# A fused Macaron block (FFN, ReLU attention, FFN) on one core: new step tables for TensorE, ScalarE, VectorE and GpSimd

## The reference

```python
x = x + 0.5 * _L0_ffn_ref(_layernorm(x), ...)      # "pre"
x = x + _L0_attn_ref(_layernorm(x), ...)           # attention, 16 heads of 8
x = x + 0.5 * _L0_ffn_ref(_layernorm(x), ...)      # "post"
# _L0_ffn_ref(x):  h = LN(x)*g + b; y = silu(h @ w1 + b1); return x + 0.5*(y @ w2 + b2)   128 -> 512 -> 128
# _L0_attn_ref(x): w = relu(q k' / sqrt(8)); attn = w / (sum(w) + 1e-6); out = (attn @ v) @ w_out + b_out
#                  return LN(x + out) * gamma + beta
```

## Time and profile before

| | |
|---|---|
| time, median of 3 runs | 376.71 us (376.18 to 376.83) |
| the profiled execution | 376.2 us, of which the span of its instructions is 374.4 us |
| PE busy | 359.7 us (96% of the span) |
| DVE, ACT, POOL busy | 279.4, 232.9, 217.7 us |
| one batch in the middle (batch 3) | 43.57 us |

### The profile page before, as it was taken

How to read it: one execution, slowest core, us unless ns; L and a number is a source line. 1 busy time by engine, 2 the same in 40 slices (tenths; PEclk the granted TensorE clock), 3 DMA queues, 4 the chain that set the end, 5 groups by cost and what they waited for, 6 DMA issues and landing times.

```text
span 374.4 us, 11752 instructions
## 1 busy us (share of the span) xinstructions
PE 359.7 (96%) x4518; PEld 182.1 (49%) x4518; DVE 279.4 (75%) x689; ACT 232.9 (62%) x425; POOL 217.7 (58%) x447
## 2 busy tenths in 40 slices
PE   8999999999999999999999999999999999999997
PEld 8844433543435544454435544455434544352376
DVE  6776678797588965888577975889658785668774
ACT  3477466656766476756777377664767567667533
POOL 7694156489734887167763787358871557014541
PEclk9999999999999999999999999999999999999999
DMA  7016006300640017200361006400270003600001
GB/s 204 10 33 167 3 6 167 83 3 2 146 108 5 3 56 165 63 4 31 77 151 30 4 28 134 122 3 3 58 194 6 2 30 70 156 4 32 0 2 60
DMA packets 14103, 22.66 MB, mean 61 GB/s; under 512 B 2528, under 2 KB 3808, under 8 KB 14048
## 3 DMA queue, kind: packets, MB, share of 16 engines
q1 hardware_dynamic: 11456, 17.83, 19.7%
q10 hardware_dynamic: 2592, 4.07, 3.3%
HBM read 3.54 MB, written 2.10 MB: 15 GB/s over the span
## 4 chain that ended last, share of the span: by engine, by line
PE 80%; DVE 10%; ACT 4%; issue 3%; POOL 2%; DMA 1%; SPq 0%; ACTq 0%; POOLq 0%; DVEq 0%
PE o_bank L685 27%; PE scores L662 13%; PE pre_bank L603 10%; PE post_bank L603 9%; DVE probs L1283 4%; PE pre_bank L608 4%; PE post_bank L608 3%; PE pre_bank L609 2%; PE pre_bank L631 2%; PE pre_bank L596 2%; PE post_bank L631 2%; PE post_bank L609 1%; PE o_bank L590 1%; ACT post_y L873 1%; ACT pre_y L873 1%
## 5 line engine op out<-in xcount | busy, mean ns | idle before, releaser
L1283 DVE TENSOR_SCALAR probs<-scores 128x512 f32<-128x512 f32 x242 | 155.1, 680 | 60.5 <-PE scores L662 56.4
L984 ACT ACTIVATE probs<-scores 128x512 f32<-128x512 f32 x262 | 141.4, 595 | 84.5 <-PE scores L662 83.2
L685 PE MATMUL o_bank<-probs,v_op 128*32 128x512 f32 x1024 | 135.8, 602 | 0.2
L662 PE MATMUL scores<-q_op,k_op 32*128 32x512 f32 x504 | 72.4, 494 | 0.8 <-ACT probs L984 0.2
L662 PEld LDWEIGHTS scores<-q_op,k_op 32*128 32x128 f32 x504 | 29.0, 181 | 72.9 <-issue 58.5
L685 PEld LDWEIGHTS o_bank<-probs,v_op 128*32 128x32 f32 x1024 | 22.3, 108 | 27.4 <-issue 23.9
L603 PEld LDWEIGHTS post_bank<-w,post_y 128*32 128x32 f32 x960 | 26.5, 110 | 12.9 <-issue 12.6
L603 PE MATMUL post_bank<-w,post_y 128*32 128x128 f32 x960 | 31.6, 273 | 0.1
L1312 POOL TENSOR_SCALAR norm_y_var<-norm_y_mv 128x4 f32<-128x4 f32 x7 | 1.4, 199 | 50.5 <-DVE norm_y_mv L1054 50.5
L603 PE MATMUL pre_bank<-w,pre_y 128*32 128x128 f32 x960 | 30.8, 274 | 0.0
L603 PEld LDWEIGHTS pre_bank<-w,pre_y 128*32 128x32 f32 x960 | 25.7, 110 | 8.1 <-issue 7.6
(11 more groups left out here) (219 smaller groups left out, 553.6 us busy)
## 6 DMA issues: line engine op xcount, KB each, us to landing
k_op<-k_parts SPq DMA_DIRECT2D x62, 128.0 KB, 2.6
q_op<-q_parts SPq DMA_DIRECT2D x62, 128.0 KB, 2.7
out_dram<-o_rows ACTq DMA_DIRECT2D x7, 256.0 KB, 2.0
pre_x<-in_x_dram ACTq DMA_DIRECT2D x6, 256.0 KB, 2.6
w_int<-in_L_ffn_fc_q_dram SPq DMA_DIRECT2D x2, 256.0 KB, 4.0
rows<-in_lines_dram ACTq DMA_DIRECT2D x1, 256.0 KB, 7.2
s_rows<-in_L_ffn_fc_scales_dram SPq DMA_DIRECT2D x1, 256.0 KB, 6.9
wqk<-in_w_qk_dram SPq DMA_DIRECT2D x1, 256.0 KB, 6.9
```

The costliest lines, as they stand in the source:

```text
L662: mm(score_bank(b, s, i, j), k_op[rows, g, P * kt:P * (kt + 1)], q_op[rows, g, :], start=True, stop=True).then_inc(scores_done[i], 1)
L685: last = mm(o_bank[pair][VW * j:VW * (j + 1), :], v_op[:, kt, heads_of(g).start + 2 * j, :], probs[:, s % 2, j, :], start=(odd == 0 and kt ...
L984: activation(probs[:, s % 2, 2 * i + j, :], score_bank(b, s, i, j), ACT.Relu).then_inc(probs_done[i][j], 1)
L1283: v.tensor_scalar(probs[:, s % 2, 2 * i + j, :], score_bank(b, s, i, j), 0.0, None, ALU.max).then_inc(probs_done[i][j], 1)
```

## The change

The matmuls and the instructions of all other engines do the same work; what changes is their order, and two waits. The tables of batches 2 to 6 (`*_ORDER`):

- PE: `fc1.1`, `fc1.2`, `fc1.3` of pre and `fc2.0` stand behind V instead of between S and V; `post.op` stands behind V and ahead of `fc1.2`; post's `fc1.2` has step 13 alone, `v` moves from step 13 to 14, and post's `fc1.3` from between S and V of step 14 to behind V of step 15.
- POOL: `x_stats` and `x_apply` of the rows after next stand behind `uT`; `post.xr`, which stood behind `uT`, stands ahead of it; `pre.xr` stands ahead of `v_in`. DVE makes its part of `x_stats` in step 10 instead of 4.

Batch 1 gets tables of its own for PE, ACT and DVE (`*_SECOND`): the same, with `post.hT` in step 8 and `post.fc1.0` to `fc1.3` in steps 9, 10, 12 and 14. The last batch does post's `fc2` in steps 0 and 1 instead of 3 to 6, ahead of `op`, and `out` and the store with it. There `op` waits for fc2's drained bank, and fc2 no longer waits for `y`.

```diff
+PE_SECOND = [
...
+    ([], ["post.hT@-1"]),
+    ([], ["post.fc1.0@-1"]),
...
 PE_ORDER = [
     ([], ["pre.fc1.0@1"]),
-    (["pre.fc1.1@1"], []),
-    (["pre.fc1.2@1", "post.op@-1"], []),
...
+    ([], ["pre.fc1.1@1"]),
+    ([], ["post.op@-1", "pre.fc1.2@1"]),
...
 PE_END = [
+    ([], ["post.fc2.0@-2"]),
+    (["post.fc2.1@-2", "post.fc2.2@-2", "post.fc2.3@-2"], []),
+    ([], ["post.op@-1"]),
...
+DVE_SECOND = [
...
+    ["oT.0", "den.0"],
+    ["post.hT@-1"],
...
 DVE_END = [
     [],
-    ["oT.1@-1", "den.1@-1", "a.1@-1", "aT@-1"],
+    ["oT.1@-1", "den.1@-1", "a.1@-1", "post.out@-2", "aT@-1"],
...
     [],
+    ["post.xr@-1"],
+    ["pre.uT@1"],
+    ["pre.x_stats@2"],
     ["pre.x_apply@2"],
-    ["pre.uT@1"],
-    ["post.xr@-1"],
-    ["pre.x1_beta@1"],
+    ["pre.x1_beta@1", "pre.xr@2"],
     ["v_in.0@1", "v_in.1@1"],
-    ["pre.xr@2"],
     [],
 ]
...
-def of_batch(b, start, order, end):
-
-    return start if b == 0 else end if b == B - 1 else order
+def of_batch(b, start, second, order, end):
+
+    return start if b == 0 else second if b == 1 else end if b == B - 1 else order
...
                         next_fill(st, b, "fc2")
-                        if st is post:
+                        if st is post and b < B - 3:
 
                             pe.wait_ge(y_done, b + 2)
...
-                            pe.wait_ge(post.free, len(POST_FILLS) * (b - 1) + post.n("fc1.3"))
+                            last_use = "fc2" if b == B - 2 else "fc1.3"
+                            pe.wait_ge(post.free, len(POST_FILLS) * (b - 1) + post.n(last_use))
```

More of the change, by code:

```diff
@@ L70 @@
 ]
+PE_SECOND = [
+    ([], ["pre.fc1.0@1"]),
+    ([], ["pre.fc1.1@1"]),
+    ([], ["post.op@-1", "pre.fc1.2@1"]),
+    ([], ["pre.fc1.3@1"]),
+    ([], ["pre.fc2.0@1"]),
+    (["pre.fc2.1@1"], ["pre.fc2.2@1"]),
+    (["pre.fc2.3@1"], []),
+    ([], []),
+    ([], ["post.hT@-1"]),
+    ([], ["post.fc1.0@-1"]),
+    (["pre.uT@1"], ["post.fc1.1@-1"]),
+    ([], ["pre.k@1"]),
+    ([], ["pre.q@1", "post.fc1.2@-1"]),
+    ([], ["pre.v@1"]),
+    ([], ["post.fc1.3@-1"]),
+    (["pre.hT@2"], []),
+]
 PE_ORDER = [
     ([], ["pre.fc1.0@1"]),
-    (["pre.fc1.1@1"], []),
-    (["pre.fc1.2@1", "post.op@-1"], []),
-    (["pre.fc1.3@1"], []),
-    (["pre.fc2.0@1"], ["pre.fc2.1@1"]),
+    ([], ["pre.fc1.1@1"]),
+    ([], ["post.op@-1", "pre.fc1.2@1"]),
+    ([], ["pre.fc1.3@1"]),
+    ([], ["pre.fc2.0@1", "pre.fc2.1@1"]),
     (["pre.fc2.2@1", "pre.fc2.3@1"], []),
@@ L84 @@
     ([], ["pre.q@1", "post.fc1.1@-1"]),
-    ([], ["pre.v@1", "post.fc1.2@-1"]),
-    (["post.fc1.3@-1"], []),
-    (["pre.hT@2"], []),
+    ([], ["post.fc1.2@-1"]),
+    ([], ["pre.v@1"]),
+    (["pre.hT@2"], ["post.fc1.3@-1"]),
 ]
@@ L141 @@
 ]
+ACT_SECOND = [
+    ["pre.fc1.0@1"],
+    ["pre.fc1.1@1"],
+    ["pre.fc1.2@1", "pre.load_x@2"],
+    ["pre.fc1.3@1"],
+    ["post.y_apply@-1"],
+    [],
+    [],
+    [],
+    ["post.hT@-1"],
+    ["post.fc1.0@-1"],
+    ["pre.uT@1", "post.fc1.1@-1"],
+    ["pre.k@1"],
+    ["pre.q@1", "post.fc1.2@-1"],
+    ["pre.v@1"],
+    ["post.fc1.3@-1"],
+    ["pre.hT@2"],
+]
 ACT_ORDER = [
@@ L155 @@
     ["pre.q@1", "post.fc1.1@-1"],
-    ["pre.v@1", "post.fc1.2@-1"],
-    ["post.fc1.3@-1"],
-    ["pre.hT@2"],
+    ["post.fc1.2@-1"],
+    ["pre.v@1"],
+    ["pre.hT@2", "post.fc1.3@-1"],
 ]
@@ L162 @@
     [],
-    [],
+    ["post.store@-2"],
     [],
@@ L167 @@
     ["post.y_apply@-1"],
-    ["post.store@-2"],
+    [],
     [],
@@ L205 @@
 ]
+DVE_SECOND = [
+    ["oT.1@-1", "den.1@-1"],
+    ["a.1@-1", "aT@-1"],
+    ["post.y@-1", "post.y_stats@-1"],
+    [],
+    [],
+    ["post.x2@-1", "post.x2_stats@-1"],
+    ["pre.x1@1"],
+    ["pre.x1_stats@1"],
+    ["oT.0", "den.0"],
+    ["post.hT@-1"],
+    ["a.0", "pre.x_stats@2"],
+    ["pre.k_lo@1"],
+    ["pre.q_lo@1"],
+    [],
+    [],
+    ["pre.hT@2"],
+]
 DVE_ORDER = [
@@ L210 @@
     [],
-    ["pre.x_stats@2"],
+    [],
     ["post.x2@-1", "post.x2_stats@-1"],
@@ L216 @@
     ["post.out@-2"],
-    ["a.0"],
+    ["a.0", "pre.x_stats@2"],
     ["post.hT@-1", "pre.k_lo@1"],
@@ L231 @@
     [],
-    ["post.out@-2"],
+    [],
     ["post.x2@-1"],
@@ L840, in _ @@
             for b in range(B):
-                for s, (early, late) in enumerate(of_batch(b, PE_START, PE_ORDER, PE_END)):
+                for s, (early, late) in enumerate(of_batch(b, PE_START, PE_SECOND, PE_ORDER, PE_END)):
                     step_scores(b, s)
@@ L975, in _ @@
             for b in range(B):
-                for s, beside in enumerate(of_batch(b, ACT_START, ACT_ORDER, ACT_END)):
+                for s, beside in enumerate(of_batch(b, ACT_START, ACT_SECOND, ACT_ORDER, ACT_END)):
                     if STEPS * b + s - 1 > 0:
@@ L1274, in _ @@
             for b in range(B):
-                for s, beside in enumerate(of_batch(b, DVE_START, DVE_ORDER, DVE_END)):
+                for s, beside in enumerate(of_batch(b, DVE_START, DVE_SECOND, DVE_ORDER, DVE_END)):
                     if STEPS * b + s - 1 > 0:
```

## The result

The changed kernel takes **384.39 us** (median of 4 runs, 383.27 to 390.37) against 376.6 us of the kernel before beside it; the ratio is **1.020** (95% interval 1.017 to 1.022). Ratios leave out two runs as slow ones: the 390.37 us here, whose granted clock was lower than that of the others, and one of 797.15 us among the twelve of experiment 6. It is slower by 7.8 us, where I had forecast 2.4 and a range that ended at 381.3. The profiled execution takes 384.3 us.

The account below looks back on a forecast made before the run. PE, busy 96% of the span, bounds the kernel, so only its waits can change. Batches 2 to 6 +4.35, batch 1 -1.0 and last batch -1.0 sum to +2.4 us on 376.71: 379.1 us, range 376.4 to 381.3.

Parts of the forecast that it names:

- the sum of step 11: Batches 2 to 6: k's new wait for POOL's low part +1.89, post's fc1.0 wait gone -0.44, restart +0.10: +1.55 us each.
- an overlap of the four large instructions with `a_t`: POOL's post.xr beside DVE's a_t: low part 0 to 0.2 us later per batch, up to +1 us in all; 0 taken.
- Batch 1: Its own tables leave 3.2 to 3.4 of 4.3 us of waits: -1.0 us, bounds -4.0 and +1.
- wait for post's low part: Batch 1: post's fc1.0, one step behind post's hT, makes PE wait some 1.6 us for DVE's low part.
- The last batch: fc2 in steps 0 and 1 covers evictions, about 1.5 us go, 1.1 come back: net -1.0 us, bounds -2 and +1.
- both silu waits: Batches 2 to 6: with quarters behind V, pre's and post's fc1 no longer wait for silu, -0.5 us each.
- the wait of k: Step 11, batches 2 to 6: PE's L755 waits for POOL's pre_t_lo, 1.5 to 2 us each.
- hT behind `v`: Batches 2 to 5: v one S ahead of hT, which waits for ACT to copy v, +0.4 us each.
- a forecast of 44.5: Sign to look for: a middle batch takes 44.5 us instead of 43.57, batch 6 a little shorter.
- The low part was not in time: Rival, chance 0.08: POOL's low part is in time, step 11 at most its old length, 371.3 us.
- nearly all its waits: Rival, chance 0.12: batch 1 loses nearly all its waits (-4.0), 376.1 us, no difference to be told.
- the bound in the middle: Rival, chance 0.12: evictions bound steps 15 to 3, 0.3 us for two steps in each batch, 382.1 us.

Follow-up runs that it names:

- experiment 6: The kernel before with the changed kernel's batch 1 tables alone, POOL's order and DVE's x_stats in step 4 as they were: 376.29 us, ratio 0.999.
- Experiment 3: The changed kernel with seven identity products between k's second and third product in batches 2 to 6, keeping PE busy: 380.75 us, ratio 1.010.
- experiment 2: The kernel before with the changed kernel's POOL order alone, DVE's tables as they were: 391.57 us, ratio 1.040.
- Experiment 5: The kernel before with the changed kernel's last-batch tables alone and the two waits that belong to them: 376.16 us, ratio 0.998.
- experiment 4: The changed kernel with v moved to step 13 and post's fc1.2 to step 14: 379.37 us, ratio 1.007.
- experiments 7: The changed kernel with low part before post.xr, v_in before pre.xr, v before post's fc1.2, x_stats in step 12, batch 1's first two post quarters one step later: 371.07 us.
- experiment 8: The changed kernel with only POOL's low part ahead of post.xr and v_in ahead of pre.xr: 374.72 us, ratio 0.995.
- experiment 1: The changed kernel with POOL's low part put back ahead of post.xr: 374.9 us, ratio 0.995.

## Why the prediction was wrong

**The step that failed** is the sum of step 11. It priced k's wait by its length alone, "+1.89 - 0.44 + 0.10 = +1.55", and had no term for the granted clock. The trace of before gave no price for it: its granted clock is 1.0 from end to end, and its longest wait of PE is 1.6 us, at the start. The forecast made five waits of 1.9 us and did not ask what else they would do. Two of the five cost 1.5 and 1.6 us more, **3.1 us**. Experiment 3 takes just this away from batches 2 to 6 and nothing else, experiment 2 brings it back in the kernel before. Without these 3.1 us the time would be 381.3, the very end of my range; experiment 3 measured 380.75.

**The same term was 0.3 us too small in each batch**, 1.4 us in all. The listed wait was 2.03 us, where I had PE 1.89 later in all; against S, k's third product comes 2.19 later, and step 11 is 1.85 us longer, not 1.55. POOL's chain ahead of the low part, 5.09 in the earlier trace rows, took 5.31 at its new place, 0.23 of it in one small instruction, held by `a_t`: 0.43 to 0.45 us in each of batches 2 to 6, 0.20 elsewhere; the other 0.09 is that it starts so much later against S. I had kept up to 0.2 for an overlap of the four large instructions with `a_t` and taken 0; the upper end was the right size, but the overlap is with the small instruction ahead of them, and the large ones took 1.76 us in batch 3, as without an overlap.

**Batch 1** was forecast at -1.0 and gave -0.2. The table alone gives -1.5 in the trace of experiment 6 and -0.5 by the median of its runs, so the gain is there and its usual size is open. The 1.5 us wait for post's low part came as forecast (1.6). What took the gain back in this execution is `a_t` held for 1.48 us (0.69 in its step), and k's wait of 0.38, which costs 0.65 in step 11 where I had the low part late by about 0.2.

**The last batch** was forecast at -1.0 and gave -0.9, in part by luck. I had fc2 in steps 0 and 1 cover the evictions of step 0. Experiment 5 has this table and S of step 0 takes 1.04 us as before; 0.54 of the 0.92 us come with batch 6's table, which has post's last quarter right ahead of this S; I had counted that move as hiding a silu and nothing more.

**Right**, with its size: both silu waits gone from batches 2 to 6; the wait of k, its place and its releaser; hT behind `v` at +0.4 (experiment 4: 0.40); batches 3 and 5, at 44.8 us, against a forecast of 44.5 that lacks only the 0.3 above; batch 6 shorter.

**The rivals.** The low part was not in time. Batch 1 did not lose nearly all its waits: it takes 41.35 us at best (experiment 6), where the rival's -4.0 asks for 38.9. Evictions did not become the bound in the middle: S groups of steps 0 to 3 stay at 0.50 or 0.51 us in batches 1 to 6 of the changed kernel. They did in the kernels of experiments 7 and 8, by a way that I had not named.

Of the 5.7 us between forecast and span (8.1 - 2.4), the clock is 3.1, the low part 1.4, batch 1 0.8. The last 0.4 are 0.48 us ahead of batch 1, partly a DMA wait (0.20 us; 0.55 in experiment 5's execution), less 0.1 us at the end.

## What to carry to other kernels

Price a new wait of the engine that bounds the kernel by its length and, if it is longer than any that the trace shows at full clock, by what the matmuls behind it cost at the lower level; give both as bounds. Before a task is put ahead of another on an in-order engine, read from the trace whether the engine was idle for the other's input, and add up the whole task. When a task is taken out of an idle stretch of such an engine, all that stands behind it comes later: see who waits for that. And when a large POOL instruction is moved, look at which DVE instructions it will lie beside, however small they are.

## What the runs showed of the hardware

**DVE and POOL exclude each other for some instructions.** In all the traces of this case, `a_t` and `den` that start while a large TENSOR_TENSOR runs on POOL end behind it: `a_t` 0.27 to 0.30 us behind its end, `den` mostly 0.04 to 0.05, whatever they would take alone (0.42 and 0.19). So `den` took from 0.19 to 1.21 us by where it fell. If DVE is first, POOL is held: 1.43 instead of 1.28 us, and 0.43 instead of 0.20. Instructions of DVE that read a bank (evictions, the low parts, `y`) kept their durations beside the same POOL instructions. The Trainium skill, SBUF — State Buffer, "SBUF: two separate sides", calls the pair of ports an exclusive lock that whoever starts first has for the whole instruction, against DVE instructions in a 2-port mode or with two SBUF inputs. The rows agree: 1.48 us for `a_t`, which has two SBUF inputs, and 1.21 for `den`, which has one; in which mode `den` runs the trace does not show. In the prediction I had weighed the Trainium skill, GPSIMD Engine Reference, Key points, which names the contention without a size, and had taken 0 to 0.2 us from one overlap; by the lock the bound for DVE is the length of POOL's instruction, 1.28 us here.

**The clock fell behind some of the 2.0 us waits and not behind others that look the same**: two of five in the changed kernel, one of five in experiment 4, three of six in experiment 2. Each fall cost 1.5 to 1.6 us. The one wait of 2.48 us, in experiment 1, had a fall behind it too. In the traces no wait of 1.5 us or less did, but the kernel of experiment 8, whose longest wait of PE behind the start is 1.48 us in its trace, shows a mean clock of 0.995 in three of its seven runs, none of them traced. The number of falls also differs between executions of one kernel: the mean granted clocks of the changed kernel's four runs are 0.991 (the traced one, with two falls), 0.974, 0.991 and 0.987. What decides it was not settled.
